# Sorted expert tiles: weights read from SBUF at a register's address, hidden rows turned on TensorE, six units' sums spread between the tiles

## Chip, core and metric

One NeuronCore of a Trainium2 chip runs the whole program. The metric is the device time of one execution in microseconds (us), as the median over runs.

## What is computed

A block of three residual parts over 128 sequences of 32 rows of 128 numbers: cross-attention over a context of 257 rows, self-attention, and a mixture of eight experts. Only the last one is touched by the change:

```
xt = layernorm(x).reshape(4096, 128)
probs = softmax(xt @ Wg)                      # Wg: 128 x 8
for each expert e: take the 512 tokens with the largest probs[:, e]
tok2exp = the best expert among those that took the token, else the best of all
out[token] = probs[token, tok2exp] * (gelu(xt @ W1[e]) @ W2[e])   # e = tok2exp[token]
x = x + out                                   # W1: 8 x 128 x 256, W2: 8 x 256 x 128
```

Each token goes through one expert, but which one is known only when the selection over all 4096 tokens is finished.

## The kernel before, in words

The 4096 tokens are 32 tiles of 128. **Dense part**: the selection is a long chain of small steps on VectorE, and while it runs TensorE doesn't wait. It takes the first 12 tiles (`DENSE`, three groups of four, `LATE`) through all eight experts, which makes 24 *units* of one group and one expert. `hidden` (L1319) makes the first product in a split of three matmuls, ScalarE applies Gelu (`gelu`, L788), `expand` (L1334) makes the second one, ScalarE copies the result out (`keep`, L797), and later, once the gates are known, VectorE adds each unit into X in four *quarters* of one tile each (`add_kept`, L1843, by `add`, L1802).

**Sorted part**: the other 20 tiles (`SORTED`) wait for the selection. GpSimd then scatters their rows to memory, sorted by expert (20 indirect DMAs, L1027), SP loads them back in five groups (L587, `GROUPS`), and they form 27 *slots* (`SLOTS`) of 128 rows. All rows of a slot have one expert, and its number is in `OWN[0, t]`, which VectorE writes (L1837). For each slot:

- `turn_rows` (L1406): TensorE turns the rows to 128 features x 128 rows; ScalarE copies that out (`evac_rows`, L810).
- `hidden_rows` (L1413): two matmuls with the slot's W1 as the stationary operand give the hidden values with the hidden unit on the partition; ScalarE applies Gelu (`gelu_rows`, L815).
- `expand_rows` (L1425): two matmuls with those hidden values as the stationary operand and W2 as the moving one.
- `add_rows` (L1849): VectorE multiplies by the gate and adds the row.
- GpSimd scatters the slot to the output (L1030 to L1036), one indirect DMA for each slot, in order.

TensorE's queue holds these in a software pipeline written out by hand: in step t `turn_rows(t)`, `hidden_rows(t - 1)`, `expand_rows(t - 2)`.

**Weights of the slots**: although all weights lie in SBUF (`w1_s`, `w2_s`), the sorted part doesn't use them. For each slot SP loads the expert's number into a register and issues two DMAs that fetch this expert's W1 and W2 from memory (`load_weights`, L571) into tiles that are free by then (`expert_w1`, `expert_w2`, L231 and L235). Slots 0 to 15 are loaded before the rows, slots 16 to 26 after them, each of those behind a wait until VectorE has added the units that lie in its place. TensorE waits for them by three semaphores, for slots 0 to 7, 8 to 15, and 16 to 26 (`WAVES`, L1419). The three stores of the dense part's rows come last in SP's queue (L590).

The queues in order: VectorE adds all 24 units and then the slots (L1854 to L1858); GpSimd has the 20 scatters and then the 27; SP has weights, rows, weights, stores.

Of the kernel before, what the change touches and what calls it, by code (L numbers as in the profile page):

```python
# [17 lines left out]
P = 128  # L18
# [8 lines left out]
SLOTS = (SORTED * P + 8 * (P - 1)) // P  # L27
# [45 lines left out]
def perceiver_block(nc, x, ctx_in, mask, Wq, bq, Wk, bk, Wv, bv, Wo, bo,  # L73
# [18 lines left out]
    with ExitStack() as ctx:  # L92
# [3 lines left out]
        def sem(name):  # L96
            return ctx.enter_context(nc.semaphore(name))
# [123 lines left out]

        WAVES = [0, 8, 16, SLOTS]
        added = [0] * 16 + [E] * 16 + [12] * 8 + [16] * 8 + [20] * 8 + [24] * 8

        def kilobyte(k):
            return QT[:, k * F:(k + 1) * F] if k < 16 else OT[:, (k - 16) * F:(k - 15) * F] if k < 32 else \
                (KB, QD, SX, SP)[(k - 32) // 8][:, (k % 8) // 2][
                    (slice(None),) + ((slice(2 * (k % 2), 2 * (k % 2) + 2),) if k < 48 or k >= 56 else
                                      (slice(8 * (k % 2), 8 * (k % 2) + 8),))]

        def expert_w1(t):  # L231
            w = kilobyte(2 * t)
            return w if t < 16 else w.rearrange("p b g q -> p (b g q)") if t < 24 else w.rearrange("p n k -> p (n k)")

        def expert_w2(t):  # L235
            w = kilobyte(2 * t + 1)
            return w if t < 16 else w.rearrange("p b g q -> p (b g q)") if t < 24 else w.rearrange("p n k -> p (n k)")

        TURNED = {2: 1, 7: 2}

        def wave_of(t):
            return sum(t >= w for w in WAVES[1:])

        XST = xn[:, 0, 0:3, :]
        HST = xg[:, :, :].rearrange("p a c -> p (a c)")[:, 0:3 * F].rearrange("p (t f) -> p t f", t=3)
        CNT, CUM, FULL = (QKR[:, k, :, :].rearrange("p a t -> p (a t)")[:, 0:E * SORTED]
                          .rearrange("p (e i) -> p e i", e=E) for k in (0, 2, 3))
# [189 lines left out]
        sent = sem("sent")  # L437
        ld_w = [sem(f"ld_w{k}") for k in range(len(WAVES) - 1)]
        ld_row = [sem(f"ld_row{k}") for k in range(len(GROUPS) - 1)]
# [73 lines left out]
        def _(sp):  # L513
# [53 lines left out]

            sp.wait_ge(s_own, 1)


            def load_weights(t):  # L571

                expert = sp.value_load(OWN[0:1, t:t + 1], min_val=0, max_val=E - 1)
                if added[2 * t + 1]:
                    sp.wait_ge(f_late, 4 * added[2 * t + 1])
                sp.dma_start(expert_w1(t), W1[bass.ds(expert, 1), :, :].rearrange("a c f -> c (a f)"))\  # L576
                    .then_inc(ld_w[wave_of(t)], 16)
                sp.dma_start(expert_w2(t).rearrange("p (j c) -> p j c", j=FC),
                             W2[bass.ds(expert, 1), :, :].rearrange("a (j f) c -> f (a j) c", f=P))\
                    .then_inc(ld_w[wave_of(t)], 16)  # L580

            for t in range(16):
                load_weights(t)
            sp.wait_ge(sent, 16 * SORTED)
            for k, (a, z) in enumerate(zip(GROUPS, GROUPS[1:])):
                dst = PAY[:, a:z, :] if a < SORTED else XSL[:, a - SORTED:z - SORTED, :]
                sp.dma_start(dst, rows_in[a * P:z * P, :].rearrange("(k p) c -> p k c", p=P)).then_inc(ld_row[k], 16)  # L587
            for t in range(16, SLOTS):
                load_weights(t)
            for g in range(LATE):  # L590
# [7 lines left out]
        def _(act):  # L598
# [216 lines left out]
            def gelu_rows(t):  # L815
                act.wait_ge(s_h, t + 1)
                wait_reuse(act, s_y, t - 2)
                nc.scalar.activation(HST[:, t % 3, :], psum[t % 4][:, 0:F], ACT.Gelu).then_inc(s_g, 1)
# [221 lines left out]
        def _(pe):  # L1040
# [353 lines left out]
            turn_dense(0)  # L1394
            router_step(1)
            for u in range(LATE * E):
# [16 lines left out]
            def hidden_rows(t):  # L1413
                pe.wait_ge(s_xt, t + 1)
                if t < 4:
                    pe.wait_ge(f_g, LATE * E * FC)
                wait_reuse(pe, s_g, t - 3)
                wave = wave_of(t)
                pe.wait_ge(ld_w[wave], 32 * (WAVES[wave + 1] - WAVES[wave]))  # L1419
                for j in range(FC):  # L1420
                    last = mm(psum[t % 4][:, j * P:(j + 1) * P],
                              expert_w1(t)[:, j * P:(j + 1) * P], XST[:, t % 3, :])
                last.then_inc(s_h, 1)
# [12 lines left out]
            for t in range(SLOTS + 2):  # L1436
# [4 lines left out]
                if t >= 2:  # L1441
                    expand_rows(t - 2)


        @block.vector
        def _(dve):
# [354 lines left out]

            def add(i, e, outputs, done):  # L1802
                for t in range(4):
# [38 lines left out]

            def add_kept(i, e):  # L1843
                dve.wait_ge(f_keep, i * E + e + 1)
                if e:
                    dve.wait_ge(f_late, 4 * (i * E + e))
                add(i, e, KEPT[i][e], f_late)

# [38 lines left out]
```

## Time and profile before

| | us |
|---|---|
| median of 3 runs | 792.52 (790.94 to 793.01) |
| the profiled execution's own time | 790.5 |
| its span, from the first to the last instruction | 788.6 |
| TensorE busy | 686.9 |
| VectorE busy | 614.0 |
| ScalarE busy | 470.3 |
| GpSimd busy | 421.1 |

Times in the views count from the start of the span. PE is TensorE's matmuls, PEld its weight loads, DVE is VectorE, ACT ScalarE, POOL GpSimd; SPq is the queue in which SP issues DMAs. A float32 matmul of the program shows as two rows, each with a weight load. The program's names in the rows are those of the memory: HT is TQ there, the hidden values of the slots (HST) are xg, the turned rows (XST) are xn, and the slots' weights lie in QT, OT, KB, QD and SX.

### The profile page before, as it was taken

Reading aid. Unit: us, or ns where it says so; the run is one execution under the profiler, and the core shown is the slowest. Engines: PE = TensorE matmul, PEld = TensorE weight load, DVE = VectorE, ACT = ScalarE, POOL = GpSimd, SP = SyncE. Lnnn points to the kernel's source line nnn. Section 1 sums busy time; section 2 is a strip of 40 time slices with the busy share of each in tenths; the row PEclk is TensorE's granted clock in tenths of the full one; section 3 lists DMA queues with packets and bytes.
Section 4 is the critical chain, followed back from the end, with each engine's and each line's share of the span. In section 5 each row is a group of like instructions: output and inputs, shape, how many; then the busy total and the mean of one; then the engine's idle time right before and its main releaser. Section 6 shows DMA issues by size and latency. Waiting matters only on the chain.

```text
span 788.6 us, 29267 instructions
## 1 busy us (share of the span) xinstructions
PE 686.9 (87%) x9979; PEld 541.7 (69%) x9979; DVE 614.0 (78%) x1437; ACT 470.3 (60%) x1499; POOL 421.1 (53%) x459
## 2 busy tenths in 40 slices
PE   4733999999999999999999957699999948999975
PEld 2422767777777777777777736488777737889874
DVE  6413989999999999999999866588888857779721
ACT  2722777777777777777777724445555424545542
POOL 4740475546545545635445129477777629606365
PEclk9985999999999999999999988689999958999988
DMA  7497444444444444444441012000000000006980
GB/s 167 102 178 173 80 91 87 90 89 86 94 92 86 97 85 97 88 89 91 85 82 39 2 38 72 1 3 4 2 0 1 4 2 0 1 2 205 278 278 24
DMA packets 195181, 60.81 MB, mean 77 GB/s; under 512 B 147556, under 2 KB 193512, under 8 KB 195122
## 3 DMA queue, kind: packets, MB, share of 16 engines
q1 hardware_dynamic: 192000, 55.65, 32.6%
q0 software_dynamic: 1824, 3.96, 1.4%
q8 instruction: 39, 0.64, 0.3%
q10 hardware_dynamic: 1298, 0.40, 0.2%
q14 instruction: 20, 0.16, 0.1%
HBM read 51.58 MB, written 8.83 MB: 77 GB/s over the span
## 4 chain that ended last, share of the span: by engine, by line
PE 52%; SPq 14%; issue 9%; ACT 8%; DVE 8%; POOL 6%; DMA 1%; ACTq 1%; POOLq 0%; DVEq 0%
PE bank L497 24%; PE energy L497 15%; PE bank L500 13%; ACT PR L660 7%; SPq L528 6%; DVE STAT L1542 3%; POOL rows_in L1027 2%; SPq L534 1%; SPq L551 1%; POOL SX L951 1%; POOL TQ L943 1%; ACTq L660 1%; SPq L576 1%; DMA MK<-in_mask_BxSxS_ik 1%; SPq L516 1%
## 5 line engine op out<-in xcount | busy, mean ns | idle before, releaser
L660 ACT ACTIVATE PR<-energy,STAT 128x256 f32<-128x256 f32 x512 | 234.4, 483 | 115.8 <-DVE STAT L1542 115.8
L1542 DVE TENSOR_REDUCE STAT<-energy 128x512 f32 (+1 forms) x256 | 164.4, 685 | 27.6 <-PE energy L497 27.5
L500 PE MATMUL bank<-ident,PR 128*128 128x128 f32 x1024 | 152.8, 283 | 30.0 <-DVE PT L1559 25.1
L1559 DVE COPY PT<-bank 128x512 f32<-128x512 f32 x256 | 162.2, 674 | 1.4 <-PE bank L500 1.4
L500 PEld LDWEIGHTS bank<-ident,PR 128*128 128x128 f32 x1024 | 110.1, 142 | 60.8 <-issue 49.4
L848 POOL TENSOR_TENSOR QB<-QT,headmask 128x512 f32<-128x512 f32 x32 | 33.3, 1039 | 191.0 <-DMA MK<-in_mask_BxSxS_ik 127.7
L660 ACT ACTIVATION_READ_ACCUMULATOR PR<-energy,STAT (+1 forms) x512 | 110.5, 216 | 0.0
L855 POOL TENSOR_SCALAR MZ<-MK 128x512 bf16<-128x512 int32 x64 | 94.2, 1487 | 6.2 <-DMA MK<-in_mask_BxSxS_ik 6.2
L497 PEld LDWEIGHTS bank<-wv_s,CT 128*128 128x128 f32 x512 | 67.9, 194 | 31.4 <-issue 31.4
L497 PE MATMUL bank<-PT,VT 128*32 128x128 f32 x2048 | 69.6, 276 | 0.0
L497 PE MATMUL bank<-wv_s,CT 128*128 128x128 f32 x512 | 68.5, 277 | 0.3 <-DVE OC L1551 0.3
L1515 DVE STREAM_TRANSPOSE CT<-CX 128x512 f32<-128x512 f32 x64 | 45.0, 703 | 29.8 <-DMA CX<-in_ctx 26.0
L497 PEld LDWEIGHTS bank<-PT,VT 128*32 128x32 f32 x2048 | 52.2, 110 | 21.2 <-DVE PT L1559 20.9
L497 PE MATMUL bank<-CT,wk_s 128*128 128x512 f32 x128 | 66.5, 602 | 0.0
L497 PE MATMUL energy<-KS,QB 32*128 32x256 f32 x1024 | 66.1, 374 | 0.0
L753 ACT ACTIVATE SX<-SX 128x512 f32<-128x512 f32 x32 | 20.2, 632 | 59.1 <-DVE SX L1680 59.1
L497 PEld LDWEIGHTS energy<-KS,QB 32*128 32x128 f32 x1024 | 49.3, 184 | 3.0
L987 POOL TENSOR_TENSOR SX<-SX,sinv 128x512 f32<-128x512 f32 x32 | 33.5, 1048 | 30.9 <-DVE sinv L1690 30.9
L861 POOL TENSOR_TENSOR OC<-OC,headmask 128x512 f32<-128x512 f32 x32 | 33.3, 1039 | 29.8 <-DVE OC L1551 29.8
L497 PE MATMUL energy<-w_s,TQ 128*128 128x128 f32 x384 | 47.6, 277 | 0.6 <-ACT TQ L794 0.6
L497 PEld LDWEIGHTS energy<-w_s,TQ 128*128 128x128 f32 x384 | 46.1, 192 | 2.1 <-ACT TQ L794 0.7
L646 ACT ACTIVATE KS<-bank,bias 128x512 f32<-128x512 f32 x64 | 46.2, 722 | 0.0
(288 smaller groups left out, 1304.8 us busy)
## 6 DMA issues: line engine op xcount, KB each, us to landing
CX<-in_ctx SPq DMA_DIRECT2D x512, 32.0 KB, 2.6
MK<-in_mask_BxSxS_ik SPq DMA_DIRECT2D x128, 128.0 KB
rows_in<-fill SPq DMA_DIRECT2D x1, 3483.0 KB, 20.1
X<-in_x SPq DMA_DIRECT2D x4, 512.0 KB, 7.7
VLT<-v_last SPq DMA_DIRECT2D x4, 512.0 KB, 9.8
QT<-in_L_ffn_W SPq DMA_DIRECT2D x16, 128.0 KB
OT<-in_L_ffn_W SPq DMA_DIRECT2D x16, 128.0 KB, 3.3
PAY<-rows_in SPq DMA_DIRECT2D x2, 903.0 KB, 7.5
```

Source lines behind the costliest of these rows:

```text
L497: return nc.tensor.matmul(o, l, r, start=start, stop=stop, skip_group_check=True)
L500: return nc.tensor.transpose(o, i, ident[0:n, 0:n])
L528: sp.dma_start(CX[rows, k, e, :, :], ctx_in[bass.ds(2 * p + e, 1), 0:KEYS, rows] .rearrange("a (n j) i -> j (a n) i", j=32)).then_inc(ld_c ...
L646: nc.scalar.activation(KS[:, k % 2, :], psum[0][:, :], ACT.Identity, bias=bias[:, 1:2])\
L660: nc.scalar.activation(PR[:, b, g, :], EB[:, g, e * KEYS:(e + 1) * KEYS], ACT.Exp, bias=STAT[:, bass.ds(t, 1), b, 1, g:g + 1].rearrange("p ...
L848: nc.gpsimd.tensor_tensor(QB[:, k, :, :, :], QT[:, bass.ds(t * P, P)].rearrange("p (b a q) -> p b a q", b=BT, a=1).broadcast_to([P, BT, 4, ...
L855: nc.gpsimd.tensor_scalar(MZ[:, k, :, :], MK[:, k, :, :], 0.0, None, ALU.is_equal).then_inc(pool_m, 1)
L861: nc.gpsimd.tensor_tensor(own, own, headmask[:, :].rearrange("p (a h c) -> p a h c", a=1, c=1).broadcast_to([P, BT, 4, SQ]), ALU.mult).the ...
L987: nc.gpsimd.tensor_tensor(SX[:, j, :, :], SX[:, j, :, :], sinv[:, j, :].rearrange("p (n a) -> p n a", a=1).broadcast_to([P, 16, SQ]), ALU. ...
L1515: V.transpose(CT[:, k % 2, :], CX[:, k, :, :, :].rearrange("p e n i -> p (e n i)")).then_inc(ev_l, 1)
L1542: V.tensor_reduce(STAT[:, bass.ds(t, 1), b:b + 2, 1, g:g + 1].rearrange("p a b g -> p (a b g)"), EB[:, g, :].rearrange("p (e k) -> p e k", ...
L1559: V.tensor_copy(PT[:, k % 2, e, 2 * half:2 * half + 2, :].rearrange("p g k -> p (g k)"), psum[1 if e else 7]).then_inc(ev_t, 1)
```

## The change

Four things:

- The DMAs of the slots' weights, their waits and `WAVES` are gone. TensorE loads the 27 expert numbers into 27 registers of its own, four after each `hidden` from unit 17 on (`FIRST_LOAD`), ahead of that unit's `expand`. In the slots it reads `w1_s` and `w2_s` at an address from the register.
- In `hidden_rows` the operands change places: the turned rows are stationary, and the expert's W1 (256 columns) is moving, in one matmul. The hidden values then come out with the row on the partition.
- So they have to be turned: after Gelu TensorE turns the two halves (`turn_hidden`) and VectorE copies 128x256 out (`evac_hidden`) to HTS, in the place of QT. The pipeline gets one step longer: in step t `turn_rows(t)`, `hidden_rows(t - 1)`, `turn_hidden(t - 2)`, `expand_rows(t - 3)`.
- VectorE adds only 18 units before the slots. The last six (`HELD`) are added a quarter at a time, one after each of the slots 0 to 23.

```diff
-        WAVES = [0, 8, 16, SLOTS]
...
+        FIRST_LOAD = 17
+        HELD = 6
...
+        HTS = QT[:, 0:3 * F].rearrange("p (t f) -> p t f", t=3)
...
-            sp.wait_ge(s_own, 1)
-            def load_weights(t):
-                expert = sp.value_load(OWN[0:1, t:t + 1], min_val=0, max_val=E - 1)
-                if added[2 * t + 1]:
-                    sp.wait_ge(f_late, 4 * added[2 * t + 1])
-                sp.dma_start(expert_w1(t), W1[bass.ds(expert, 1), :, :]...).then_inc(ld_w[wave_of(t)], 16)
-                sp.dma_start(expert_w2(t)..., W2[bass.ds(expert, 1), :, :]...).then_inc(ld_w[wave_of(t)], 16)
-            for t in range(16):
-                load_weights(t)
             sp.wait_ge(sent, 16 * SORTED)
...
-            for t in range(16, SLOTS):
-                load_weights(t)
...
             def gelu_rows(t):
                 act.wait_ge(s_h, t + 1)
-                wait_reuse(act, s_y, t - 2)
+                wait_reuse(act, s_turned, t - 2)
...
+            def load_experts(n):
+                if not own:
+                    pe.wait_ge(s_own, 1)
+                for t in range(len(own), min(len(own) + n, SLOTS)):
+                    own.append(pe.value_load(OWN[0:1, t:t + 1], min_val=0, max_val=E - 1))
...
+                if u >= FIRST_LOAD:
+                    load_experts(4)
                 expand(u // E, u % E, between)
...
                 wait_reuse(pe, s_g, t - 3)
-                wave = wave_of(t)
-                pe.wait_ge(ld_w[wave], 32 * (WAVES[wave + 1] - WAVES[wave]))
-                for j in range(FC):
-                    last = mm(psum[t % 4][:, j * P:(j + 1) * P],
-                              expert_w1(t)[:, j * P:(j + 1) * P], XST[:, t % 3, :])
+                wait_reuse(pe, s_ht, t - 3)
+                last = mm(psum[t % 4][:, 0:F], XST[:, t % 3, :],
+                          w1_s[:, bass.ds(own[t], 1), :].rearrange("p a f -> p (a f)"))
                 last.then_inc(s_h, 1)
+            def turn_hidden(t):
+                pe.wait_ge(s_g, t + 1)
+                for j in range(FC):
+                    last = tr(psum[t % 4][:, F + j * P:F + (j + 1) * P], HST[:, t % 3, j * P:(j + 1) * P])
+                last.then_inc(s_turned, 1)
             def expand_rows(t):
-                pe.wait_ge(s_g, t + 1)
+                pe.wait_ge(s_ht, t + 1)
...
-                    last = mm(psum[4 + t % 2][:, 0:P], HST[:, t % 3, j * P:(j + 1) * P],
-                              expert_w2(t)[:, j * P:(j + 1) * P],
+                    last = mm(psum[4 + t % 2][:, 0:P], HTS[:, t % 3, j * P:(j + 1) * P],
+                              w2_s[:, bass.ds(own[t], 1), j, :].rearrange("p a c -> p (a c)"),
...
+            def evac_hidden(t):
+                dve.wait_ge(s_turned, t + 1)
+                wait_reuse(dve, s_y, t - 2)
+                V.tensor_copy(HTS[:, t % 3, :], psum[t % 4][:, F:2 * F]).then_inc(s_ht, 1)
...
-            for i in range(LATE):
-                for e in range(E):
-                    add_kept(i, e)
-            for t in range(SLOTS):
-                add_rows(t)
+            for u in range(LATE * E - HELD):
+                add_kept(u // E, u % E)
+            for t in range(SLOTS + 1):
+                if t < SLOTS:
+                    evac_hidden(t)
+                if t:
+                    add_rows(t - 1)
+                u = LATE * E - HELD + t // 4
+                if u < LATE * E:
+                    add_kept(u // E, u % E, [t % 4])
```

## Rows read from the trace of the kernel before

**Rows 1.** Waits, 735 to 789 us: who waited for whom, total us, times, longest.

```profile
PE bank L497 <- DMA SX<-in_L_ffn_W: 5.3, 1, 5.3
POOL out L1033 <- DVE PAY L1851: 15.4, 9, 10.3
POOL out L1033 <- issue: 4.9, 16, 0.3
```

**Rows 2.** Timeline of POOL: start us, us, instruction, idle time before it and its releaser.

```profile
735.98 0.96 POOL L1027 DMA_INDIRECT rows_in<-PAY,SLOT  x1 [0.30 <-issue]
747.21 1.00 POOL L1033 DMA_INDIRECT out<-PAY  x1 [10.28 <-DVE PAY L1851]
765.27 0.98 POOL L1033 DMA_INDIRECT out<-PAY  x1 [0.30 <-issue]
768.63 0.98 POOL L1033 DMA_INDIRECT out<-PAY  x1 [2.37 <-DVE PAY L1851]
770.54 0.98 POOL L1033 DMA_INDIRECT out<-PAY  x1 [0.94 <-DVE PAY L1851]
771.83 0.98 POOL L1033 DMA_INDIRECT out<-PAY  x1 [0.30 <-DVE PAY L1851]
783.42 0.98 POOL L1033 DMA_INDIRECT out<-XSL  x1 [0.31 <-issue]
```

**Rows 3.** Timeline of the start of the slots, all engines, 738 to 746 us.

```profile
737.94 3.73 PE L497 MATMUL energy<-w_s,TQ 128*128 128x128 f32 x32
739.46 4.87 DVE L1805 SCALAR_TENSOR_TENSOR X<-SP,GATE,X 128x128 f32<-128x128 f32 x16
738.40 0.41 SPq L578 DMA_DIRECT2D OT<-in_L_ffn_W  x1
740.01 2.05 SPq L587 DMA_DIRECT2D PAY<-rows_in  x4
743.08 0.44 PE L500 MATMUL bank<-ident,PAY 128*128 128x128 f32 x2 [1.41 <-DMA PAY<-rows_in]
744.68 0.33 PE L500 MATMUL bank<-ident,PAY 128*128 128x128 f32 x1 [0.19 <-DMA PAY<-rows_in]
745.04 0.28 ACT L813 ACTIVATE xn<-bank 128x128 f32<-128x128 f32 x1
745.95 0.35 DVE L1851 SCALAR_TENSOR_TENSOR PAY<-energy,PAY 128x128 f32<-128x128 f32 x1 [1.61 <-PE energy L497]
```

**Rows 4.** Timeline of PE in the steady slots: one slot from turn to turn.

```profile
750.76 0.27 PE L500 MATMUL bank<-ident,PAY 128*128 128x128 f32 x1
750.87 0.61 PE L497 MATMUL energy<-xn,QT 128*128 128x128 f32 x4
751.31 0.61 PE L497 MATMUL energy<-QT,xg 128*128 128x128 f32 x4
751.76 0.27 PE L500 MATMUL bank<-ident,PAY 128*128 128x128 f32 x1
```

**Rows 5.** Timeline of PE in cross-attention: two passes of 512 columns, and what follows.

```profile
299.84 1.02 PE L497 MATMUL bank<-CT,wk_s 128*128 128x512 f32 x2
300.70 1.05 PE L497 MATMUL bank<-wv_s,CT 128*128 128x128 f32 x8
```

**Rows 6.** One line's durations (min/median/max ns): the 128x256 copy, the row scatters.

```profile
L1773 DVE COPY SEL<-bank x1: 424/424/424, 701.3 to 701.3; 128x256 f32<-128x256 f32 x1
L1027 POOL DMA_INDIRECT rows_in<-PAY,SLOT x20: 956/960/1218, 711.6 to 736.0; - x20
```

**Rows 7.** Timeline of SP: the issues of one slot's two weight DMAs, and the next.

```profile
715.01 0.39 SPq L578 DMA_DIRECT2D QT<-in_L_ffn_W  x1
716.16 0.34 SPq L576 DMA_DIRECT2D QT<-in_L_ffn_W  x1
716.60 0.38 SPq L578 DMA_DIRECT2D QT<-in_L_ffn_W  x1
```

**Rows 8.** Stretches: busy us (x count) of PE, PEld, DVE, ACT, POOL; granted clock; DMA share, GB/s.

```profile
560.45:564.35 3.90, 3.84 (x116) 3.08 (x116) 3.16 (x9) 1.96 (x5) 2.65 (x4) 1.00 0.00 0
708.70:711.87 3.17, 3.17 (x23) 2.91 (x22) 2.90 (x11) 1.79 (x4) 0.31 (x1) 1.00 0.02 5
```

More of the change, by code:

```diff
@@ L220, in group_of @@
             return sum(t >= g for g in GROUPS[1:])
-        WAVES = [0, 8, 16, SLOTS]
[L223 to L237, printed above, removed]
         TURNED = {2: 1, 7: 2}
-        def wave_of(t):
-            return sum(t >= w for w in WAVES[1:])
+        FIRST_LOAD = 17
+        HELD = 6
         XST = xn[:, 0, 0:3, :]
         HST = xg[:, :, :].rearrange("p a c -> p (a c)")[:, 0:3 * F].rearrange("p (t f) -> p t f", t=3)
+        HTS = QT[:, 0:3 * F].rearrange("p (t f) -> p t f", t=3)
         CNT, CUM, FULL = (QKR[:, k, :, :].rearrange("p a t -> p (a t)")[:, 0:E * SORTED]
@@ L437, in perceiver_block @@
         sent = sem("sent")
-        ld_w = [sem(f"ld_w{k}") for k in range(len(WAVES) - 1)]
+        s_turned = sem("s_turned")
+        s_ht = sem("s_ht")
         ld_row = [sem(f"ld_row{k}") for k in range(len(GROUPS) - 1)]
@@ L566, in store @@
                 sp.dma_start(out_tiles[:, bass.ds(g * 4, 4), :], X[:, bass.ds(g * 4, 4), :]).then_inc(st_out, 16)
-            sp.wait_ge(s_own, 1)
-            def load_weights(t):
-                expert = sp.value_load(OWN[0:1, t:t + 1], min_val=0, max_val=E - 1)
-                if added[2 * t + 1]:
-                    sp.wait_ge(f_late, 4 * added[2 * t + 1])
[L576 to L580, printed above, removed]
-            for t in range(16):
-                load_weights(t)
             sp.wait_ge(sent, 16 * SORTED)
@@ L1395, in _ @@
             router_step(1)
+            own = []
+            def load_experts(n):
[3 more added lines that the diff above has]
+                    own.append(pe.value_load(OWN[0:1, t:t + 1], min_val=0, max_val=E - 1))
             for u in range(LATE * E):
@@ L1417, in hidden_rows @@
                 wait_reuse(pe, s_g, t - 3)
-                wave = wave_of(t)
-                pe.wait_ge(ld_w[wave], 32 * (WAVES[wave + 1] - WAVES[wave]))
+                wait_reuse(pe, s_ht, t - 3)
+                last = mm(psum[t % 4][:, 0:F], XST[:, t % 3, :],
+                          w1_s[:, bass.ds(own[t], 1), :].rearrange("p a f -> p (a f)"))
+                last.then_inc(s_h, 1)
+            def turn_hidden(t):
+                pe.wait_ge(s_g, t + 1)
                 for j in range(FC):
-                    last = mm(psum[t % 4][:, j * P:(j + 1) * P],
-                              expert_w1(t)[:, j * P:(j + 1) * P], XST[:, t % 3, :])
-                last.then_inc(s_h, 1)
+                    last = tr(psum[t % 4][:, F + j * P:F + (j + 1) * P], HST[:, t % 3, j * P:(j + 1) * P])
+                last.then_inc(s_turned, 1)
             def expand_rows(t):
-                pe.wait_ge(s_g, t + 1)
+                pe.wait_ge(s_ht, t + 1)
                 if t < 2:
@@ L1430, in expand_rows @@
                 for j in range(FC):
-                    last = mm(psum[4 + t % 2][:, 0:P], HST[:, t % 3, j * P:(j + 1) * P],
-                              expert_w2(t)[:, j * P:(j + 1) * P],
+                    last = mm(psum[4 + t % 2][:, 0:P], HTS[:, t % 3, j * P:(j + 1) * P],
+                              w2_s[:, bass.ds(own[t], 1), j, :].rearrange("p a c -> p (a c)"),
                               start=(j == 0), stop=(j == FC - 1))
                 last.then_inc(s_y, 1)
-            for t in range(SLOTS + 2):
+            for t in range(SLOTS + 3):
                 if t < SLOTS:
@@ L1440, in _ @@
                     hidden_rows(t - 1)
-                if t >= 2:
-                    expand_rows(t - 2)
+                if 0 <= t - 2 < SLOTS:
+                    turn_hidden(t - 2)
+                if t >= 3:
+                    expand_rows(t - 3)
         @block.vector
@@ L1800, in _, with add @@
             link(gates(DENSE, NT))
-            def add(i, e, outputs, done):
-                for t in range(4):
+            def add(i, e, outputs, done, quarters=range(4)):
+                for t in quarters:
                     xi = X[:, bass.ds(i * 4 + t, 1), :].rearrange("p a c -> p (a c)")
@@ L1841, in _, with add_kept @@
             dve.wait_ge(t_done, 1)
-            def add_kept(i, e):
+            def add_kept(i, e, quarters=range(4)):
                 dve.wait_ge(f_keep, i * E + e + 1)
                 if e:
-                    dve.wait_ge(f_late, 4 * (i * E + e))
-                add(i, e, KEPT[i][e], f_late)
+                    dve.wait_ge(f_late, 4 * (i * E + e) - 3 + quarters[-1])
+                add(i, e, KEPT[i][e], f_late, quarters)
+            def evac_hidden(t):
+                dve.wait_ge(s_turned, t + 1)
+                wait_reuse(dve, s_y, t - 2)
+                V.tensor_copy(HTS[:, t % 3, :], psum[t % 4][:, F:2 * F]).then_inc(s_ht, 1)
             def add_rows(t):
```

## Prediction

> **What bounds the kernel now.** I read the end first, since whatever doesn't move the last instruction is worth nothing. The waits of the last 54 us show one large stall on TensorE, 5.3 us for the weights of slots 16 to 26 [rows 1], and it invites the reading that the change is worth 5.3 us. The timeline of POOL says otherwise. The last thing to run is its 27 output scatters: the first starts at 747.21, the last at 783.42 and ends at 784.40; the span ends 4.2 us later at 788.6. Where nothing is late, one scatter follows another at (783.42 - 771.83) / 9 = 1.288 us [rows 2], 0.98 of work and 0.30 of issue, and 16 of the 27 wait for nothing but issue [rows 1]. A slot costs TensorE only 1.00 us, from turn to turn [rows 4]. So POOL lags behind TensorE, and much of the 5.3 us is eaten by that lag: what reaches POOL is a gap of 2.37 and one of 0.94 in place of 0.30 each, 2.71 us [rows 2]. That is the most that the stall itself can give back. After that the end is the start of the first scatter plus 26 x 1.288 + 0.98 = 34.47 us, whatever TensorE does, as long as a slot takes it less than 1.288 us.
>
> The start of the slots then decides. The dense part's last matmul is issued out at 737.94 + 3.73 = 741.67. The sorted rows come later: the last row scatter is issued by 736.94 [rows 2], SP sees it landed and issues the row loads at 740.01, and TensorE gets the first two slots at 743.08 and slot 2 at 744.68 [rows 3]. So TensorE has 1.4 us of slack there, and POOL's 20 row scatters set the time.
>
> **The change, part by part.**
>
> *Weight DMAs and the third semaphore's wait go.* Gain at POOL: 2.71 us. In SP's queue only the row loads and the three stores are left. The first two stores follow the row loads at once, at about 742, and move beside loads of rows that are due ten slots later.
>
> *Does less DMA traffic bring the rows earlier?* The last row scatter needs 3.07 us from the end of its issue until SP moves on, with weight DMAs issued beside it until 738.81; the first row load needs 3.07 us too [rows 2, 3]. Not shown is either without company. Bounds: 0, and 1.5 us if a quarter of both waits were queueing. I take 0.3, near the low end, since a load that takes 3 us for 258 KB, and less than two more for the next 516 KB, is mostly latency.
>
> *TensorE's slot.* Before: 9 passes in 1.00 us, 0.111 each [rows 4]. Now turn 1 x 0.111, first product 2 passes of 256 columns, two turns 2 x 0.111, second product 4 x 0.111. A pass of 512 columns takes (300.70 - 299.84) / 2 = 0.43 [rows 5], so 256 take 0.215, and the slot 0.11 + 0.43 + 0.22 + 0.44 = 1.21 us. That is under 1.288: it costs nothing after the first slot, and the cover is POOL's scatter.
>
> *VectorE's slot.* Copy 0.42 [rows 6], add 0.35 [rows 3], and in slots 0 to 23 one quarter of a held unit, 4.87 / 16 = 0.304 [rows 3]: 1.08 us. The copy waits for the turn, the add for the second product 0.44 later, so from the turn's end 0.25 + 0.42 + 0.35 + 0.30 = 1.32, against a next copy that comes due at 1.21 + 0.25. It fits, with 0.14 us to spare. ScalarE does what it did. Behind VectorE's new wait for the turn stand the add that POOL needs and the held quarter, which nobody needs before the third store; that store is issued at about 774 and hidden under the scatters.
>
> *Holding six units back.* VectorE ended its sums at 739.46 + 4.87 = 744.33 [rows 3], before the first copy comes due (below). Alone it gives nothing, and costs nothing while the slot fits.
>
> *One step more before the first slot is done.* Before: row 0 added at 746.30, scatter at 747.21, 0.91 later [rows 2, 3]. Now, with rows as late as before: slot 2 is turned at 744.68; first product of slot 1 until 745.22 (0.11 + 0.43); turn of slot 0 until 745.44; VectorE sees it 0.25 later (a turn started at 744.68 was read by ScalarE at 745.04, which is 0.36 from its start) and copies until 746.11. TensorE goes on with 0.76 us of slots 3, 2 and 1 until 746.20 and the second product of slot 0 until 746.64. VectorE copies slot 1 and adds row 0 from 746.89 to 747.24. So the first scatter is 0.94 us later. This is a cost that nothing hides.
>
> *27 register loads on TensorE, four in each of units 17 to 23.* The trace of before has none there, so I bound them. SP's queue has the same load: between the end of one slot's second DMA issue, 715.40, and the next slot's first, 716.16, lie 0.76 us; between the two issues of a slot, 0.10 [rows 7]. So a load with its address arithmetic takes at most 0.76, some 0.66 without the issue gap. If all of it stops the array: 27 x 0.76 = 20.5 us; if the array works off what was queued meanwhile: 0. Which is nearer? A dense unit feeds the array 22 matmuls in 3.17 us; a tile of self-attention feeds it 116 in 3.90, 0.034 each with a weight load each, at the same full clock [rows 8]. So the sequencer needs about 22 x 0.034 = 0.75 us of a unit's 3.17, and 2.4 are free for four loads (2.6 to 3.0 at SP's price, less if the address arithmetic comes only later, as here it does). Ahead of the loads stands a whole `hidden`, 3.17 - 16 x 0.111 = 1.4 us of array work, behind them an `expand` that must wait for Gelu anyway. I take 0: the free time is nearly the whole price, the slack before the rows (1.1 us after the 0.3) takes what sticks out, and the row with the sequencer's own rate is nearer than SP's. Address arithmetic also stands ahead of three matmuls in each slot; self-attention's loop has register addresses too (L1241, L1292), inside its 0.034.
>
> The Trainium skill, "Runtime: NRT & Kernel Launch", section "Instruction fetch mechanics", puts a register load from memory at about 200 ns. By that, as an estimate, all 27 would be 5.4 us, and hidden the more easily; no run here shows it.
>
> **Sum**, against the profiled execution: -2.71 (stall) + 0.94 (longer pipeline) - 0.3 (rows earlier) = -2.1 us. Its own time is 790.5 for a span of 788.6, and it lies 2.0 under the median of the runs, 792.52. The difference is carried over to the median: 790.4.
>
> A measurement of this kernel can tell about 0.3%, 2.4 us, from no change. The forecast of -2.1 lies just inside.
>
> **Rivals.**
>
> *A. TensorE's register loads stop the array (the slower side).* Place: ahead of `expand` in units 17 to 23. For it: the sequencer issues in order, and four loads at SP's price (2.6 to 3.0) with 0.75 of other work exceed a unit's 3.17 by 0.22 to 0.62, times seven 1.5 to 4.3 us, less 1.1 of slack: the sum becomes -1.7 to +1.1, 790.8 to 793.6. If nothing is queued ahead at all, 17.8 to 20.5 less 1.1: 807 to 810. It decides from the point where the dense part ends over 1.1 us later than 741.67, and turns the sign when it ends 3.2 later. Against it: the sequencer's rate above. Chance 0.18.
>
> *B. The rows come much earlier.* At the bound of 1.5 us the sum is -3.3, 789.2. The dense part's end at 741.67 permits it just so. Chance 0.08.
>
> *C. A slot takes over 1.288 us.* POOL then waits for every row, and each 0.1 us over that is 2.6 us: a slot of 1.4 gives -2.1 + 2.9 = +0.8, 793.3, one of 1.5 gives +3.4, 795.9. The place is VectorE's 0.14 us to spare. Chance 0.06.
>
> *D. VectorE's new work slows POOL's scatters.* They would now share the time with copies and sums. If each of the first 24 had to wait for one held quarter of 0.304, that is +7.3 on -2.1: 797.7. Against it: the 20 row scatters ran beside back-to-back sums of the same kind at a median of 0.960 us, the output scatters beside a nearly idle VectorE at 0.98 [rows 2, 6]. The Trainium skill, "SBUF — State Buffer", section "SBUF: two separate sides", says that GpSimd and VectorE share a port pair as an exclusive lock and that a DMA issued by GpSimd can starve behind it. By that rule this change is a danger; the trace doesn't agree, with 0.960. Chance 0.05.
>
> **How the numbers follow.** The forecast as it stands has 0.63; its own range is 789.5 to 791.6, from the bounds of the earlier rows and half a microsecond on the first slot. Some two fifths of it lie beyond -2.4: 0.24 faster, 0.39 same. B adds 0.08 faster. A is slower with 0.13 and same with 0.05; C and D are slower with 0.10 and same with 0.01. Faster 0.32, same 0.45, slower 0.23. The range reaches from 788.9 (B and the scatter of the runs) to 795.0, over the milder half of A and C, and leaves out A in full and D.
>
> **What the changed profile would show.** Right: scatters 1.288 apart from the first to the last with no gap; the first one at 747.5 to 748.2; TensorE's slots 1.21 apart with no wait for a DMA; the clock at 1.00 throughout; the dense part ending near 741.7. Wrong: idle time of TensorE put down to issue between 719 and 742 (A); a first scatter before 747 (B); gaps at POOL released by VectorE (C); scatters longer than 0.98 (D).

## The result, and the profile after

The kernel after takes 786.32 us against 792.52: a ratio of 0.9935 [0.9911, 0.9959]. The forecast was 790.4 with a range from 788.9, so the time lies 2.6 us below the range. Two later comparisons gave 0.9954 [0.9925, 0.9984] and 0.9953 [0.9929, 0.9977]; in those the forecast's own ratio, 790.4 / 792.52 = 0.9973, lies inside. The sign is sure; the size is 3.6 to 5.2 us by the three ratios.

The profiled execution of after took 787.4 us, its span is 785.5. I read its end first, as with before. These are the waits from 735 us on of POOL's output scatters and of TensorE's matmuls (total us, times, longest):

```profile
POOL out L998 <- DVE PAY L1837: 12.7, 5, 11.5
POOL out L998 <- issue: 5.2, 17, 0.3
POOL out L998 <- DVE XSL L1837: 1.5, 5, 0.3
PE bank L480 <- ACT xn L778: 0.7, 1, 0.7
```

TensorE's 5.3 us for a DMA [rows 1] have no successor: its longest wait is 0.7 us, and for ScalarE. The timeline of POOL (first and last row scatter, then output scatters):

```profile
709.84 1.22 POOL L992 DMA_INDIRECT rows_in<-PAY,SLOT  x1 [21.90 <-DVE SLOT L1814]
...
734.22 0.96 POOL L992 DMA_INDIRECT rows_in<-PAY,SLOT  x1 [0.30 <-issue]
746.66 1.00 POOL L998 DMA_INDIRECT out<-PAY  x1 [11.48 <-DVE PAY L1837]
747.96 0.99 POOL L998 DMA_INDIRECT out<-PAY  x1 [0.31 <-issue]
...
780.34 0.98 POOL L998 DMA_INDIRECT out<-XSL  x1 [0.30 <-issue]
```

From the first output scatter to the end of the last are 780.34 + 0.98 - 746.66 = 34.66 us, no gap among them over 0.31, where before had 784.40 - 747.21 = 37.19 [rows 2]. The start of the slots, SP's row loads and TensorE:

```profile
736.84 2.06 SPq L554 DMA_DIRECT2D PAY<-rows_in  x4
737.43 4.08 PE L480 MATMUL energy<-w_s,TQ 128*128 128x128 f32 x32
741.35 0.38 PE L483 MATMUL bank<-ident,PAY 128*128 128x128 f32 x2
742.47 0.69 PE L480 MATMUL bank<-w_s,xn 128*128 x2 [0.73 <-ACT xn L778]
743.00 0.27 PE L483 MATMUL bank<-ident,PAY 128*128 128x128 f32 x1
```

Two things differ from [rows 3]. The row loads go out 1.66 us after the last row scatter's end (735.18), where it was 3.07. And the first turn has no wait for a DMA behind it: it follows the dense part's last matmuls, which take 4.08 us for what took 3.73. So TensorE, no longer the rows, sets the start of the slots.

Executions of one and the same kernel begin this end at very different times (the first row scatter lies between 709.8 and 716.4), with the same code ahead of it in both kernels. So from here on I measure each trace from its first row scatter to the end of its last output scatter: **the stretch**. After it the span has 4.1 to 4.2 us left in every trace. On the two traces just read the stretch is 784.40 - 711.56 = 72.84 before and 781.32 - 709.84 = 71.48 after: 1.4 us.

### The profile page after: what moved, and what is told of

It reads as the page before. It is cut to its first block, busy times and chain, and to the rows that moved or that the text cites. A ratio compares the mean times of both kernels' runs of the same rounds, so it can differ in the third digit from the quotient of the medians.

```text
span 785.5 us, 29282 instructions
## 1 busy us (share of the span) xinstructions
PE 689.4 (88%) x9979; PEld 541.1 (69%) x9979; DVE 624.1 (79%) x1464; ACT 470.1 (60%) x1499; POOL 421.5 (54%) x459
## 4 chain that ended last, share of the span: by engine, by line
PE 60%; SPq 9%; issue 8%; ACT 8%; DVE 7%; POOL 5%; ACTq 1%; DMA 1%; DVEq 0%; POOLq 0%
PE bank L480 25%; PE energy L480 20%; PE bank L483 14%; ACT PR L625 7%; SPq L511 5%; DVE STAT L1523 3%; SPq L534 1%; SPq L517 1%; POOL SX L916 1%; POOL TQ L908 1%; ACTq L625 1%; POOL MZ L820 1%; DMA MK<-in_mask_BxSxS_ik 1%; PE energy L483 1%; SPq L499 1%
## 5 line engine op out<-in xcount | busy, mean ns | idle before, releaser
L1523 DVE TENSOR_REDUCE STAT<-energy 128x512 f32 (+1 forms) x256 | 164.1, 684 | 27.1 <-PE energy L480 27.1
```

What stands on the lines that cost most here:

```text
L1523: V.tensor_reduce(STAT[:, bass.ds(t, 1), b:b + 2, 1, g:g + 1].rearrange("p a b g -> p (a b g)"), EB[:, g, :].rearrange("p (e k) -> p e k", ...
```

## The experiments

Theory **W**: the weight DMAs cost before its third wave and the late rows, and everything that the change gains lies in the stretch. Theory **L**: the register loads take part of it back, on TensorE. Rival **H**: the six units held back are what helps. Rival **N**: the difference between the kernels is chance from run to run.

**Both kernels again.** No edit.

> The kernel before, unchanged, so that a second trace of it stands beside the first. Question: how much of the 5 us between the two kernels lies ahead of the slots, where nothing was changed. Theory N (run to run): the first row scatter starts anywhere within about 2 us of 711.56, while the stretch from the first row scatter to the end of the last output scatter is 72.8 us again, within 0.3. Rival V (the stretch itself varies): that stretch differs by over 1 us from 72.8, through the wait for the weights of slots 16 to 26. Ratio to the kernel before 1.000 within 0.003.

> The changed kernel, unchanged. Theory N: first row scatter within about 2 us of 709.84, then 71.5 us until the end of the last output scatter, within 0.3; ratio 0.990 to 0.997, centred on 0.9935. Rival V: the stretch is 70.5 or less, so that the first trace of it was a long one.

Before against itself: 1.0002 [0.9975, 1.0029]; after: 0.9954 [0.9925, 0.9984]. N falls as an account of the whole difference. The stretch is 72.71 in the one and 71.43 in the other.

**Register loads replaced by constants.**

```diff
-                if not own:
-                    pe.wait_ge(s_own, 1)
...
-                    own.append(pe.value_load(OWN[0:1, t:t + 1], min_val=0, max_val=E - 1))
+                    own.append(t * E // SLOTS)
```

> The changed kernel with the 27 expert numbers written into the program in place of the register loads (it leaves out the choice of the expert for each slot), so that nothing but the loads and the address arithmetic goes. Theory L (the loads stretch the dense part by 1.5 us, and this sets when the slots start): units 17 to 23 take 3.17 us each again, TensorE is through with them about 31.9 us after the first row scatter's start in place of 31.7 + 1.5, slot 0 is turned when its rows have landed, about 1.4 us earlier, and the stretch from the first row scatter to the end of the last output scatter falls from 71.5 to about 70.1; ratio some 0.002 lower than that of the changed kernel. Rival R (the rows set it): the stretch stays at 71.5, TensorE waits for a DMA at slot 0.

Ratio 0.9942 [0.9913, 0.997]. The stretch is 69.80, 1.6 us under after. The first row scatter is at 714.56, and the timeline of TensorE has the last `expand` so:

```profile
740.96 3.73 PE L480 MATMUL energy<-w_s,TQ 128*128 128x128 f32 x32
```

So the dense part ends 30.13 us after the first row scatter, as in before (30.11), where after has 31.67. The edit takes out TensorE's wait for the numbers (`s_own`) as well; the next run keeps that wait and has the same stretch within 0.2, so it is not the wait. L stands: the loads cost what the dense part ends later. What they are in the trace of after is shown by the list of the loads' line (min/median/max ns, on TensorE's sequencer):

```profile
L1367 PEldq TENSOR_LOAD <-OWN x27: 293/301/714, 717.7 to 738.8; - x27
L1367 PEldq FUSED_REGOPS  x27: 146/146/165, 718.4 to 739.1; - x27
L1367 PEldq SEQ_ASSERT  x27: 18/18/26, 718.7 to 739.3; - x27
```

A load with its address arithmetic and its check of the bounds is 0.301 + 0.146 + 0.018 = 0.465 us, and 27 are 12.6. Of these 1.5 reach the array. The timeline of TensorE shows where:

```profile
720.14 0.40 PE L480 MATMUL bank<-XH,W1H 128*128 128x512 f32 x1
720.82 2.02 PE L480 MATMUL energy<-w_s,TQ 128*128 128x128 f32 x16 [0.28 <-ACT TQ L759]
...
727.66 2.02 PE L480 MATMUL energy<-w_s,TQ 128*128 128x128 f32 x16 [0.18 <-ACT TQ L759]
```

The array has run dry ahead of `expand`, which stands behind the four loads. The trace puts these gaps down to Gelu; with constants, and the same Gelu, they are gone. From the start of the last `hidden` matmul to that of `expand` it is 0.68 and 0.58 us here, 0.23 to 0.24 with constants. With the 4.08 for 3.73 at the end, these three places make 1.1 of the 1.5 us; the other units lose some 0.1 each.

**The same 27 loads, one at a time.** Each stands in one of the last 28 gaps between the matmuls of the dense part, in the function that puts other work there too.

```diff
             def between():
                 passed[0] += 1
+                if passed[0] > 4 * LATE * E - SLOTS - 1:
+                    load_experts(1)
...
-                if u >= FIRST_LOAD:
-                    load_experts(4)
```

> The changed kernel with the same 27 register loads, but one at a time, at four places in each unit (after each half of hidden and after every second quarter of expand) in place of four together ahead of expand. Theory L: a load with its arithmetic takes 0.46 us and stands ahead of 0.7 us or more of array work, so it is hidden; the dense part is at most 0.3 us longer than without loads, the slots start 1.2 to 1.5 us earlier, and the stretch falls from 71.5 to about 70.2, as with fixed experts. Rival S (each load stops the array for its own time wherever it stands): 27 x 0.46 = 12.6 us are not hidden in any place, and since 1.5 are seen with four together, the stretch is 71.5 again or longer.

Ratio 0.9927 [0.9896, 0.9958]. The loads take as long (median 302 ns), but the timelines of TensorE and POOL read as with constants:

```profile
737.13 3.73 PE L480 MATMUL energy<-w_s,TQ 128*128 128x128 f32 x32
740.70 0.38 PE L483 MATMUL bank<-ident,PAY 128*128 128x128 f32 x2
...
746.01 1.00 POOL L998 DMA_INDIRECT out<-PAY  x1 [9.88 <-DVE PAY L1837]
...
779.69 0.98 POOL L998 DMA_INDIRECT out<-XSL  x1 [0.30 <-issue]
```

The last `expand` is back at 3.73. The first row scatter is at 710.75, so the stretch is 780.67 - 710.75 = 69.92. What the loads cost is thus a matter of how they are placed, four together or one at a time, and not of their sum.

**Before without any weight DMA.** Its slots read `w1_s` and `w2_s` at fixed experts; everything else is before's.

```diff
         def expert_w1(t):
-            w = kilobyte(2 * t)
-            return w if t < 16 else ...
+            return w1_s[:, t * E // SLOTS, :]
...
-            for t in range(16):
-                load_weights(t)
...
-            for t in range(16, SLOTS):
-                load_weights(t)
...
-                pe.wait_ge(ld_w[wave], 32 * (WAVES[wave + 1] - WAVES[wave]))
```

> The kernel before without any of the slots' weight DMAs: TensorE reads W1 and W2 from where they lie in SBUF all along, at fixed addresses, in the old pipeline (it leaves out the choice of the expert for each slot). Theory D (the weight DMAs delay the last row scatter by 1.4 us and stall slot 16): from the first row scatter's start, the row loads are issued at 27.0 in place of 28.5, TensorE turns slot 0 at about 30.2 (its dense part ends at 30.1), the first output scatter starts at about 34.3, and the stretch to the end of the last is 34.3 + 34.7 = 69.0 in place of 72.8. In the median of the runs about 3.8 us less. Rival S (something else that came with the change shifts the stretch ahead of the slots too): the median falls by 5.5 or more, as the runs of the changed kernel lie some 2 us lower than their stretch says.

Ratio 0.994 [0.9913, 0.9967], stretch 68.68, where theory D expected 69.0. The gain by the ratio, 4.8 us, lies under the 5.5 of rival S, but its interval, 2.6 to 6.9, doesn't exclude it. SP's row loads and the row scatter ahead of them (started at 738.25) stand so in the timelines of POOL and SP:

```profile
738.25 0.96 POOL L1007 DMA_INDIRECT rows_in<-PAY,SLOT  x1 [0.30 <-issue]
741.02 2.06 SPq L569 DMA_DIRECT2D PAY<-rows_in  x4
```

That is 741.02 - 739.21 = 1.81 us, in before's own program, where the trace of the prediction has 3.07. What held the rows up has two sides, and this run takes both away. One is a late landing beside the weights' traffic: in the trace of the prediction SP is through with its weights at 738.81 [rows 3] and then waits 1.20 us until the last row scatter has landed. The other is SP's own queue. In the fifth trace of before the last row scatter ends at 736.77, and SP is still busy with weights:

```profile
739.12 0.38 SPq L578 DMA_DIRECT2D OT<-in_L_ffn_W  x1
739.55 2.22 SPq L587 DMA_DIRECT2D PAY<-rows_in  x4
```

Over before's nine traces SP goes from its last weight to the rows in 0.05 us (two), 0.3 to 0.5 (four) and 1.0 to 1.4 (three). How much each side costs by itself was not measured. TensorE and VectorE have the old slots here, so the gain of 68.68 against before needs nothing of what the change adds.

**Before without the third wave only.** Slots 16 to 26 take the weights of slots 0 to 10.

```diff
         def expert_w1(t):
+            t %= 16
...
-            for t in range(16, SLOTS):
-                load_weights(t)
```

> The kernel before with the weight DMAs of slots 0 to 15 only; slots 16 to 26 use the weights of slots 0 to 10 (so their expert is another). Only the third wave's DMAs and the stall go. Theory D: row loads still at 28.5, first output scatter still at about 35.7, no gap at GpSimd, stretch 35.7 + 34.7 = 70.3, so 2.4 to 2.7 us less than 72.8. Rival: with the rows loaded beside less traffic the first scatter comes over 0.5 us earlier as well, and the stretch is under 69.8.

Ratio 0.9975 [0.9948, 1.0002], stretch 71.68: no gap over 0.35 between output scatters, but the row loads still go out 28.63 us after the first row scatter and the first output scatter is at 37.15. The expectation missed by 1.4 us: it took the first output scatter, 35.7, from a trace with an early one. Against before's mean of 73.45 (below) the third wave costs 73.45 - 71.68 = 1.8 us, the start the other 71.68 - 68.68 = 3.0.

**After with the first 16 slots' weight DMAs put back**, into memory that nobody reads.

```diff
+            for t in range(16):
+                expert = sp.value_load(OWN[0:1, t:t + 1], min_val=0, max_val=E - 1)
+                if t >= 6:
+                    sp.wait_ge(f_late, 4 * (E if t < 14 else 12))
+                sp.dma_start(place[2 * t], W1[bass.ds(expert, 1), :, :]...).then_inc(ld_w, 16)
+                sp.dma_start(place[2 * t + 1]..., W2[bass.ds(expert, 1), :, :]...).then_inc(ld_w, 16)
             sp.wait_ge(sent, 16 * SORTED)
```

> The changed kernel with the weight DMAs of 16 slots added back to SP's queue ahead of the row loads, into memory that nobody reads. Theory D: the row loads are issued at 28.5 in place of 27.0 from the first row scatter, slot 0 is turned at 31.5 to 32 in place of 31.5, since the rows then come about when TensorE is through with its dense part at 31.6, and the stretch is 71.5 to 72.0. Rival Q (the row scatters were late in the kernel before because SP was busy, and not through DMA traffic): the same, with the row loads at 27.0 whenever SP is through with its DMAs by then.

Ratio 1.0021 [0.9993, 1.005]: the whole gain is gone. The stretch is 74.10, and only its start has changed; the 27 scatters still take 34.66 us. The timelines of POOL and SP:

```profile
737.90 0.96 POOL L1004 DMA_INDIRECT rows_in<-PAY,SLOT  x1 [0.30 <-issue]
742.92 0.38 SPq L561 DMA_DIRECT2D KB<-in_L_ffn_W  x1
743.36 2.13 SPq L566 DMA_DIRECT2D PAY<-rows_in  x4
```

The expectation, row loads at 28.5 and a stretch of 71.5 to 72.0, missed: they go out at 29.85. This run doesn't separate traffic from queue either: SP itself is busy with the last of the weights until 743.30, which is 4.44 us behind the last row scatter where before's traces have 1.7 to 3.3, and the rows stand behind them. So it prices the DMAs higher than before does. It shows that after gains nothing if they stay in this form.

**After with no unit held back.**

```diff
-        HELD = 6
+        HELD = 0
```

> The changed kernel with no unit held back: VectorE adds all 24 units ahead of the slots. Theory of the prediction (holding back gives nothing): VectorE is through with unit 23 at about 33.7 us from the first row scatter's start (its result is copied out at about 32.3 and four adds take 1.3), slot 0 is there to be copied at 34.3, so first output scatter 36.8 and stretch 71.4 to 71.5, as with six held back. Rival B (VectorE has a backlog when the slots start): the first copy comes late, and the first output scatter by as much, 0.5 us or more.

Ratio 0.9962 [0.9944, 0.9979], stretch 71.30 against 71.4. H falls: in the stretch of this one trace, holding six units neither gives nor costs more than 0.2 us.

**How much the stretch of one kernel varies.** The unchanged kernels again, since single traces of before did not agree.

> The kernel before, unchanged, for a third trace. Two traces gave a stretch of 72.8 and 72.7 us from the first row scatter to the end of the last output scatter, but both belong to executions faster than the median. Theory N (run to run scatter lies ahead of the slots): 72.7 within 0.3 again, whatever the execution's own time. Rival V (the stretch of the kernel before varies with the time of its weight DMAs): over 73.5 in an execution that is slower than 792.

> The kernel before, unchanged, for a fourth trace. The first three have stretches of 72.84, 72.71 and 74.01 us in executions of 790.5, 788.95 and 796.44 us. Rival V (the slots' stretch of the kernel before varies, because its row loads and weight DMAs share the DMA engines): between 72.5 and 75.5, with the first output scatter between 35.6 and 37.5 and the gaps at GpSimd of changing length. Theory N: 72.8 within 0.3, and the third was an exception.

> As for the fourth trace of the kernel before: V 72.5 to 75.5 with a changing first scatter and changing gaps; N 72.8 within 0.3.

> The changed kernel, unchanged, for a third trace. Its first two have 71.48 and 71.43. V (only the kernel with weight DMAs varies): 71.45 within 0.2 again. N (any kernel's stretch varies now and then by 1 us): over 71.8 or under 71.1.

> The kernel before, unchanged, for more traces of its stretch. If the stretch holds what is missing, the mean of these four is 74.5 or more; if not, it is 73.3 again within 0.5.

> As for the sixth trace: 74.5 or more in the mean of four if the stretch holds what is missing, 73.3 within 0.5 if not.

> As for the sixth trace: 74.5 or more in the mean of four if the stretch holds what is missing, 73.3 within 0.5 if not.

> As for the sixth trace: 74.5 or more in the mean of four if the stretch holds what is missing, 73.3 within 0.5 if not.

Worked out from the timelines, us, each from the trace's first row scatter:

| | stretch | row loads issued | first output scatter |
|---|---|---|---|
| before, nine traces | 72.60 to 74.53, mean 73.45 | 28.2 to 28.7 | 35.6 to 38.5 |
| after, four traces | 71.41 to 71.48 | 27.0 to 27.1 | 36.7 to 36.8 |
| loads one at a time, two traces | 69.92, 69.96 | 27.0 | 35.3 |

After repeats itself to 0.1 us, before spreads over 1.9. The execution's own time doesn't tell the stretch: the ninth, the second fastest at 790.3 us, has 74.10. Two things vary at the start of the slots. One is when the rows land: by the lists of DMA issues the second row load (516 KB) takes 4.2 to 6.3 us from issue to landing in before's nine traces, 3.9 to 4.2 in after's four. The other is the granted clock behind the wait for them. The fifth trace of before (stretch 74.17) has both; TensorE at the start of its slots, by its timeline:

```profile
743.48 0.44 PE L500 MATMUL bank<-ident,PAY 128*128 128x128 f32 x2 [1.97 <-DMA PAY<-rows_in]
...
746.44 0.48 PE L500 MATMUL bank<-ident,PAY 128*128 128x128 f32 x1 [1.55 <-DMA PAY<-rows_in]
746.70 1.06 PE L497 MATMUL bank<-xn,QT 128*128 128x128 f32 x4
747.56 1.06 PE L497 MATMUL energy<-QT,xg 128*128 128x128 f32 x4
748.41 0.42 PE L500 MATMUL bank<-ident,PAY 128*128 128x128 f32 x1
```

The windows of the same execution (busy us and counts of PE, PEld, DVE, ACT, POOL; granted clock; DMA share, GB/s):

```profile
743.39:745.39 2.00, 1.15 (x6) 0.73 (x6) 0.78 (x3) 0.83 (x3) 0.00 (x0) 1.00 1.05 359
745.39:747.39 2.00, 0.95 (x5) 0.96 (x6) 0.00 (x0) 0.28 (x1) 0.00 (x0) 0.52 1.08 354
747.39:749.39 2.00, 2.00 (x11) 2.00 (x11) 0.35 (x1) 0.66 (x2) 0.00 (x0) 0.50 1.10 354
```

TensorE waits 1.97 and 1.55 us for rows, and then the clock is at 0.50, the level of 1.2 GHz: four passes take 1.06 instead of 0.61 [rows 4], and from turn to turn it is 1.97 us instead of 1.00. That is over POOL's 1.288, so POOL waits for rows in its turn. Against the trace of the prediction slot 2 is turned 1.93 us later (35.05 after the first row scatter, not 33.12), which is the rows; from there to the first output scatter it is 3.49 instead of 2.53, and that 0.96 is the clock. The trace that the prediction read has the same thing behind the wait for the third wave, which its windows show:

```profile
759.56:761.56 2.00, 0.49 (x5) 0.25 (x3) 0.35 (x1) 0.63 (x2) 1.39 (x3) 1.00 0.75 224
761.56:763.56 2.00, 0.00 (x0) 0.00 (x0) 0.00 (x0) 0.00 (x0) 1.70 (x2) 0.76 0.68 202
763.56:765.56 2.00, 0.23 (x1) 0.26 (x2) 0.00 (x0) 0.00 (x0) 1.39 (x3) 0.50 0.90 276
765.56:767.56 2.00, 2.00 (x10) 2.00 (x11) 0.14 (x1) 0.38 (x1) 0.70 (x1) 0.50 0.98 293
```

In all nine traces of before the slots have some time at 0.50, behind one of these waits or behind both. The three that by their windows have the most of it, some 10 us against some 7, have stretches of 74.0 to 74.5; the fifth, with 74.17, has some 7, so the clock alone does not order them. The Trainium skill, "TensorE: Matmul & The Clock Gate", section "HAM oscillation — how this bites in real kernels", has this case: a wait for a DMA throttles the array again, and the work behind it starts slow. The trace agrees, with 0.50 behind 1.97 and 1.55 us; not every wait here does it, since the clock stays at 1.00 behind 1.41 us in the trace of the prediction [rows 3], and behind 1.18 and 0.89 us with the DMAs put back. The windows of after show none of it at the start, and none in the steady slots:

```profile
741.84:743.84 2.00, 1.37 (x7) 0.95 (x8) 0.00 (x0) 1.29 (x6) 0.00 (x0) 1.00 1.09 364
743.84:745.84 2.00, 2.00 (x15) 1.78 (x14) 1.56 (x5) 1.22 (x4) 0.00 (x0) 1.00 1.08 354
...
750.00:760.00 10.00, 10.00 (x76) 9.19 (x75) 8.62 (x26) 5.28 (x17) 7.56 (x9) 1.00 0.20 63
```

**Is there a gain outside the stretch?** After is 73.45 - 71.44 = 2.0 us shorter in the stretch, the paired runs say 3.3 and more.

> The kernel after once more, unchanged. By the theory that all the gain lies between the first row scatter and the last output scatter: that stretch is 71.4 us again, against a mean of 73.5 in nine traces of the kernel before, so the times should lie 2.0 us under those of before on this chip, a ratio near 0.9975. By the rival, that something outside this stretch gains as well: 3.3 to 5.3 us, a ratio of 0.9933 to 0.9958.

> The kernel after with its register loads spread over the dense part's last 28 gaps, once more. By the theory that all the gain lies in the stretch: 69.9 us there, 3.5 us under before, a ratio near 0.9956, and 1.5 us under the kernel after in the same call. By the rival, that something outside gains as well: 4.8 to 6.8 us under before, a ratio of 0.9914 to 0.994.

After: 0.9953 [0.9929, 0.9977], in the rival's range; loads one at a time: 0.9941 [0.9918, 0.9964], a hair above it. The lower ends of the gain, 792.71 x 0.0023 = 1.8 and x 0.0036 = 2.9 us, take in the stretch's 2.0 and 3.5, the middles lie 1.2 to 1.7 beyond. **This stays open.** Nothing ahead of the stretch tells the kernels apart: the first row scatter starts at 712.3 in the mean of before's nine traces and at 711.4 in after's four, where single traces of before spread over 6. The last four traces of before have a mean stretch of 73.7, within their expectation for a stretch that does not hold what is missing. The nine traced executions of before also average 791.8, under the 793.3 of its 21 runs in this comparison, so stretches of over 73.45 may be commoner in the untraced ones; that can't be read from a trace. Against a fixed gain of after's code outside the stretch speaks the run with the DMAs put back, which has that code and is 1.7 us slower than before (-0.6 to 4.0) with a stretch 0.65 longer. The two variants of before agree with their stretches: 4.8 us by the ratio and 4.8 by the stretch without DMAs, 2.0 and 1.8 without the third wave.

## Why the prediction was wrong in size

The chain that it worked with was right: POOL's scatters set the end, 27 of them cost 34.66 (forecast 34.47), and only what reaches the first scatter or opens a gap counts. Three steps failed: the rows come 1.4 us earlier and not 0.3, the loads cost 1.5 us and not 0, and a difference worked out from one execution of before was added to the median. Its terms, against the one trace that it used:

| step | forecast | measured |
|---|---|---|
| third wave's stall at POOL | -2.71 | 37.19 to 34.66: -2.53 |
| rows earlier | -0.3 | row loads -1.45, first turn 0.0 |
| 27 register loads | 0 | dense part ends +1.5 |
| one step more before the first slot | +0.94 | first turn to first scatter 4.13 to 5.31: +1.18 |
| sum (the rows and the loads meet in the first turn and count once, 0.0) | -2.1 | -1.4 |

- **The stall.** Right, and the reading of it against TensorE's 5.3 too. What the step left out is the clock: it took the gap of 0.94 [rows 2] for part of the wait, and it is a slot at 0.50 behind it, with TensorE's turns 769.09 - 767.17 = 1.92 us apart and 0.98 of that POOL's own work.
- **Rows earlier: 0.3 of 1.5 taken, 1.4 it was.** The step lumped two waits together as "mostly latency". For the first row load that holds: 3.0 us from issue to landing in the trace of the prediction, 2.9 in after. For the last row scatter it failed: without weight DMAs beside it SP moves on after 1.66 us, not 3.07. The Trainium skill, "Trainium Kernel Development and Optimization", section "Key Constraints", says that DMAs of SP's and POOL's queues run on the same 16 engines and interleave. By that the upper bound was the nearer end; the trace agrees as far as it goes, with 1.66 against 3.07, but in other traces of before SP's own queue has a share that was not measured apart. Rival B, rows at the bound, thus came true in SP's queue and not in the time, since the loads stood in its way.
- **Register loads: 0 taken, 1.5 it was.** The step compared averages: 2.4 us of sequencer time free in a unit against four loads. Four loads were 4 x 0.465 = 1.86, less than that. But ahead of them the array had only the 1.4 us of a `hidden` to work off, a number that the step names and then doesn't set against the price. That the work queued ahead is what counts fits the run with the loads spread and two units, but it is not shown. By it six units would lose 1.86 - 1.4 = 0.46 us each, and the last, with three loads behind a whole `expand` (16 x 0.111 = 1.8), nothing; two lost some 0.4, four some 0.1, and the last 0.35. What sets the loss of a unit stays open. Rival A had place and mechanism, and a partial price of 1.5 to 4.3. Its point of decision, 1.1 us of slack, was computed with rows that came 0.3 earlier; as they came 1.4 earlier, the slack was nearly nil, and the two misses cancelled in this trace to 0.0 at the first turn, by luck. The 200 ns that the Trainium skill, "Runtime: NRT & Kernel Launch", section "Instruction fetch mechanics", gives for a register load from memory were not met by this one, from SBUF: 301, plus 164 around it.
- **One step more.** Right in kind, 0.2 too small. From slot 2's turn to the end of row 0's add it was 745.74 - 743.00 = 2.74 us, worked out as 2.56; from add to scatter 0.92, as taken. The sign that the forecast gave, a first output scatter at 747.5 to 748.2, is 35.9 to 36.6 us from the first row scatter; it was 36.8.
- **Slots, VectorE, six units.** Right. In after's steady slots TensorE turns 1.21 us apart, and VectorE has 0.15 to spare (forecast 0.14), which its timeline shows:

```profile
757.02 0.42 DVE L1833 COPY QT<-energy 128x256 f32<-128x256 f32 x1 [0.15 <-PE energy L483]
757.47 0.35 DVE L1837 SCALAR_TENSOR_TENSOR PAY<-energy,PAY 128x128 f32<-128x128 f32 x1
757.74 0.34 DVE L1786 SCALAR_TENSOR_TENSOR X<-SP,GATE,X 128x128 f32<-128x128 f32 x1
758.23 0.42 DVE L1833 COPY QT<-bank 128x256 f32<-128x256 f32 x1 [0.15 <-PE bank L483]
```

- **Rival C** (slot over 1.288) and **rival D** (scatters slowed by VectorE) didn't come. D is worth at most 0.2: two of the 27 scatters take 1.06 and 1.08, and none does with no unit held back. The port lock that the forecast cites did not show in the 0.98 of the others.
- **Carried over to the median: the step that cost the range.** The sum was made against a stretch of 72.84, and before's mean is 73.45; the low end allowed for rows, but for no execution of before in which rows land later and the clock falls at the start as well. That is 0.6 us of the miss. Against the mean, the stretch gives 2.0 of gain: the forecast's 2.1, by two errors that cancel and a base that was too short, so the agreement is luck. The rest of the first comparison, 5.2 us of gain by the ratio against 2.0, lies partly in its five runs a side: those of after are 785.44 to 787.57, while the same kernel's later medians, of 12 runs each, are 790.35 and 789.27, inside the forecast's range, beside 793.41 and 792.71 for before. The later runs give 3.3 to 3.7 in the means; what lies beyond 2.0 stays open.

So of before's weight DMAs, which cost 73.45 - 68.68 = 4.8 us of stretch, the change gets 2.0 back. 1.5 goes to the loads, the rest to the longer way of a slot (35.26 - 34.20 = 1.1 to the first scatter, with the loads spread) and to the scatters (0.2). **Spreading the loads gives the shortest stretch of the kernels here that read the expert numbers**: 0.9927 and 0.9941 against before, and 1.5 us less stretch than after; in the runs beside it the medians lie 3.3 and 1.8 us under after's, with intervals that overlap.

## What to carry to other kernels

Whether register loads in a busy engine's queue are hidden could not be told from the time free on average: 27 of them cost 1.5 us in fours and nothing one at a time, so spread them. A wait for a DMA can cost more than its length, since the clock may be at half behind it, as in all nine traces of before; the kernel without these waits repeated itself to 0.1 us. And before a forecast is hung on a single trace, look whether what is to be removed is the very thing that varies between executions.

## What was not expected of the hardware

- From the end of POOL's last row scatter until SP moved on took 1.66 us in after, 1.81 in before without weight DMAs, and 3.07 in before with them, of which SP was idle for 1.20; row loads of 516 KB landed 4.2 to 6.3 us after their issue in before, 3.9 us with the weight DMAs gone.
- A register load from SBUF on TensorE's sequencer took 0.301 us, 0.465 with its address arithmetic and its check of the bounds; 27 of them cost 1.5 us in fours and none when spread.
- In the fifth trace of before the clock stood at 0.50 behind waits of 1.97 and 1.55 us for rows. In the trace that the forecast read it stayed at 1.00 behind the 1.41 us at the same place [rows 3], so one trace of before did not show what this wait can cost.
